# Expert tiles of a fused decoder layer: gate and up product with the weights held and the tokens moving

## The reference

```python
combine = (one_hot(topk_idx, 16) * topk_w[..., None]).sum(1)      # 4 of 16 experts per token
def step(acc, ew):                                                # per expert, I = 176
    w_gu, w_d, cw = ew                                            # (352, 256), (256, 176), weight per token
    gu = x @ w_gu.T
    h = silu(gu[:, :176]) * gu[:, 176:]
    return (acc + h @ w_d.T * cw[:, None], None)
```

## Time and profile before

| | |
|---|---|
| median of 3 runs | 620.12 us |
| profiled execution, its own time | 620.9 us |
| its span, first to last instruction | 619.1 us |
| TensorE matmul busy (PE) | 582.2 us, 94% |
| weight loads (PEld) | 457.3 us, 74% |
| VectorE (DVE) | 492.9 us, 80% |
| ScalarE (ACT) | 415.8 us, 67% |
| POOL | 396.7 us, 64% |
| mean granted TensorE clock | 0.986 of full speed |

### The profile page before, as it was taken

One profiled execution on the slowest core, in us unless ns is written; L12 is line 12 of the kernel. 1 busy time (PEld: TensorE's weight loads), 2 busy tenths in 40 slices (PEclk: granted clock), 3 DMA queues, 4 the chain that ended last, 5 costly groups with the idle time before them and its releaser, 6 DMA issues.

```text
span 619.1 us, 18771 instructions
## 1 busy us (share of the span) xinstructions
PE 582.2 (94%) x5883; PEld 457.3 (74%) x5883; DVE 492.9 (80%) x1516; ACT 415.8 (67%) x1060; POOL 396.7 (64%) x439
## 2 busy tenths in 40 slices
PE   7789899999999999999999999978899999999991
PEld 2558779889888897898888888966467667676760
DVE  4558798989979989899878768577567789989883
ACT  4877977877868768878678586432266666666661
POOL 1147868888888878878788878696100456545553
PEclk9999999999999999999999999899899999999996
DMA  7826324334233233153202111012444677877753
GB/s 228 281 78 179 104 87 137 87 104 155 80 128 106 82 123 115 67 158 113 100 2 96 45 44 53 19 35 87 145 120 137 179 222 217 238 220 226 225 164 115
DMA packets 55682, 78.95 MB, mean 128 GB/s; under 512 B 7330, under 2 KB 46370, under 8 KB 55588
## 3 DMA queue, kind: packets, MB, share of 16 engines
q1 hardware_dynamic: 37300, 48.51, 25.9%
q0 software_dynamic: 6912, 18.88, 10.2%
q10 hardware_dynamic: 11376, 10.36, 4.9%
HBM read 44.43 MB, written 33.29 MB: 126 GB/s over the span
## 4 chain that ended last, share of the span: by engine, by line
PE 81%; POOL 6%; issue 6%; ACT 2%; DVE 2%; DMA 1%; POOLq 0%; DVEq 0%; ACTq 0%
PE ps L776 11%; PE ps L660 9%; PE ps L555 7%; PE ps L588 6%; PE ps L486 5%; PE ps L682 5%; PE ps L788 5%; PE ps L799 4%; PE ps L543 4%; PE ps L608 4%; PE ps L592 3%; PE ps L765 3%; PE ps L526 2%; POOL kv_lo L1491 2%; PE ps L516 2%
## 5 line engine op out<-in xcount | busy, mean ns | idle before, releaser
L1491 POOL TENSOR_TENSOR kv_lo<-kv,kv_hi 128x512 f16<-128x512 f32 x64 | 79.6, 1245 | 30.2 <-ACT kv_hi L914 29.9
L1562 POOL DMA_INDIRECT toeplitz_lo<-y_slots,slots x44 | 43.3, 983 | 81.3 <-DMA y_slots<-kv 57.3
L776 PE MATMUL ps<-w_gate_up_hi,toeplitz_hi 128*128 x316 | 83.6, 313 | 0.4 <-DVE toeplitz_hi L1399 0.4
L1530 POOL DMA_INDIRECT x_slots<-x_norm,slots x64 | 69.2, 1080 | 18.8 <-issue 14.4
L1479 POOL TENSOR_TENSOR kv<-ctx_t_sb,v_t 128x512 f32<-128x512 f32 x64 | 69.2, 1091 | 15.9 <-ACT v_t L903 15.8
L883 ACT ACTIVATE probs<-ps,row_neg_max 128x128 f32<-128x128 f32 x256 | 71.8, 393 | 1.1 <-DVE row_neg_max L1091 0.9
L555 PEld LDWEIGHTS ps<-v_ones,probs_t 128*128 128x128 f32 x512 | 62.2, 192 | 2.2
L555 PE MATMUL ps<-v_ones,probs_t 128*128 128x17 f32 x512 | 60.7, 256 | 0.0
L588 PE MATMUL ps<-kv_hi,toeplitz_hi 128*128 128x128 f16 x256 | 56.5, 221 | 3.2 <-POOL kv_lo L1491 1.7
L1000 ACT ACTIVATE toeplitz_hi<-ps 128x256 f16<-128x256 f32 x79 | 30.3, 384 | 43.4 <-ACT stage L1019 17.9
L588 PE MATMUL ps<-kv_lo,toeplitz_hi 128*128 128x128 f16 x256 | 56.3, 220 | 0.0
(11 more groups left out here) (226 smaller groups left out, 2074.8 us busy)
## 6 DMA issues: line engine op xcount, KB each, us to landing
stage<-in_w_units SPq DMA_DIRECT2D x36, 512.0 KB, 3.8
x_slots<-zeros SPq DMA_DIRECT2D x15, 512.0 KB
toeplitz_hi<-x_slots SPq DMA_DIRECT2D x40, 128.0 KB
y_slots<-stage ACTq DMA_DIRECT2D x40, 128.0 KB
y_slots<-kv ACTq DMA_DIRECT2D x39, 128.0 KB
kv_hi<-x_slots SPq DMA_DIRECT2D x20, 128.0 KB
x_slots<-zeros SPq DMA_DIRECT2D x1, 2432.0 KB
kv_lo<-x_slots SPq DMA_DIRECT2D x19, 128.0 KB
```

The source lines that it names most:

```text
L776: last = nc.tensor.matmul(psum[2 + t % 2][:, 0:2 * INTER], bxT[a][t % 2][:, kc, :], egu[b][:, bass.ds(e, 1), kc, :].rearrange("p a n -> p ...
L1491: nc.gpsimd.tensor_tensor(flat(kvh[1][g % 2]), kv[g % 2][:].rearrange("p h j i -> p (h j i)"), flat(kvh[0][g % 2]), ALU.subtract).then_inc ...
L1530: pool.indirect_dma_start(out=xbuf, out_offset=bass.IndirectOffsetOnAxis(ap=slots[:, row, j:j + 1], axis=0), in_=xn[2][row % 2][:], in_off ...
L1562: pool.indirect_dma_start(out=yg[n][j], out_offset=None, in_=ybuf[0:(last_tile(row, j) + 1) * P], in_offset=bass.IndirectOffsetOnAxis(ap=s ...
```

## The change

Gate and up are made the other way round: the weights are held and the tokens move, so that the inner index lies on the partitions and `turn_inner` goes. The 352 weight columns of an expert are laid out anew on the host as gate 0 to 111, up 0 to 111, up 112 to 175, gate 112 to 175, and are used as three held blocks of 112, 128 and 112 columns, each against 2 chunks and 3 products: 18 matmuls of 128 moving columns. The gate goes through the Silu function on ScalarE in two instructions; VectorE multiplies with up in two instructions and writes to PSUM, from which the split in halves goes on as before. The inner index 112 to 175 stands there twice, on partitions 0 to 63 and 64 to 127, since the down product takes these rows once with the high and once with the low weights. The orders of ScalarE and VectorE are turned: the split of tile s-2 now stands ahead of the gate of tile s-1. A Silu of one column is put ahead of the stage on ScalarE.

```diff
@@ gate_up, turn_inner, down_tile (TensorE)
                 e = experts[t]
-                for kc in range(KC):
-                    for a, b, first, end in products(kc == 0, kc == KC - 1):
-                        last = nc.tensor.matmul(psum[2 + t % 2][:, 0:2 * INTER], bxT[a][t % 2][:, kc, :],
-                                                egu[b][:, bass.ds(e, 1), kc, :].rearrange("p a n -> p (a n)"),
-                                                start=first, stop=end)
+                to = psum[2 + t % 2]
+                for at, n, col in ((0, IN_A, 0), (2 * IN_A, 2 * IN_B, P), (IN_A, IN_A, 2 * P)):
+                    for kc in range(KC):
+                        for a, b, first, end in products(kc == 0, kc == KC - 1):
+                            last = nc.tensor.matmul(to[0:n, col:col + P],
+                                                    egu[b][:, bass.ds(e, 1), kc, at:at + n].rearrange("p a n -> p (a n)"),
+                                                    bxT[a][t % 2][:, kc, :], start=first, stop=end, skip_group_check=True)
                 last.then_inc(t_gu.sem, 1)
-
-            def turn_inner(t):
-                if t < 2:
-                    emptied(4 + t)
-                t_inner.wait(pe, t)
-                t_hlo.wait(pe, t - 2)
-                to, h = psum[4 + t % 2], bhh[t % 2]
-                for c in range(2):
-                    last = nc.tensor.transpose(to[:, c * P:(c + 1) * P], h[:, c * P:(c + 1) * P], id_sb[:])
-                last.then_inc(t_hT.sem, 1)
...
-                for piece, behind in ((turn_x, 0), (gate_up, 1), (turn_inner, 2), (down_tile, 3)):
+                for piece, behind in ((turn_x, 0), (gate_up, 1), (down_tile, 3)):
@@ ScalarE
+            nc.scalar.activation(sink[:], minus_half[:], ACT.Silu)
...
-                t_ga.wait(act, t - 2)
-                nc.scalar.activation(bth[t % 2], psum[2 + t % 2][:, 0:INTER], ACT.Tanh, scale=0.5 / WS)\
-                    .then_inc(t_th.sem, 1)
+                t_inner.wait(act, t - 2)
+                if t == 0:
+                    act.wait_ge(s_set, 14)
+                to, g = bsg[t % 2], psum[2 + t % 2]
+                nc.scalar.activation(to[0:IN_B, 0:P], g[IN_B:P, P:2 * P], ACT.Silu, scale=1.0 / WS)
+                nc.scalar.activation(to[0:IN_A, P:2 * P], g[0:IN_A, 0:P], ACT.Silu, scale=1.0 / WS).then_inc(t_sg.sem, 1)
...
-                for piece, behind in ((x_hi, 0), (gate_th, 1), (inner_hi_tile, 2), (y_out, 3)):
+                for piece, behind in ((x_hi, 0), (inner_hi_tile, 2), (gate_silu, 1), (y_out, 3)):
@@ VectorE (the three instructions of gate_tile go)
+            def inner_tile(t):
...
+                t_sg.wait(dve, t)
+                t_hlo.wait(dve, t - 2)
+                to, g, sg = psum[4 + t % 2], psum[2 + t % 2], bsg[t % 2]
+                nc.vector.scalar_tensor_tensor(out=to[0:IN_A, 0:2 * P], in0=g[0:IN_A, P:3 * P], scalar=1.0 / WS,
+                                               in1=sg[0:IN_A, :], op0=ALU.mult, op1=ALU.mult).then_inc(t_in.sem, 1)
+                t_in.wait(dve, t)
+                nc.vector.scalar_tensor_tensor(out=to[IN_B:P, 0:P], in0=g[0:IN_B, P:2 * P], scalar=1.0 / WS,
+                                               in1=sg[0:IN_B, 0:P], op0=ALU.mult, op1=ALU.mult).then_inc(t_inner.sem, 1)
...
-                for piece, behind in ((x_lo, 0), (gate_tile, 1), (inner_lo_tile, 2)):
+                for piece, behind in ((x_lo, 0), (inner_lo_tile, 2), (inner_tile, 1)):
```

More of the change, by code:

```diff
@@ L21 @@
 EXPERTS, TOP, INTER, SHARED = 16, 4, 176, 704
+IN_A, IN_B = 112, 64
 NB = 16
@@ L251, in build @@
         acc = [st[:, 1024 + n * E:1024 + (n + 1) * E] for n in range(2)] + [z_mem[:, TOP * E:(TOP + 1) * E]]
-        bth = [st[:, 1536 + n * INTER:1536 + (n + 1) * INTER] for n in range(2)]
-        bga = [st[:, 1888 + n * INTER:1888 + (n + 1) * INTER] for n in range(2)]
-        bhh = [st[:, 2240 + n * E:2240 + (n + 1) * E] for n in range(2)]
+        bsg = [st[:, 2240 + n * E:2240 + (n + 1) * E] for n in range(2)]
+        sink = sb("table_sink", [P, 1])
         psum = [stack.enter_context(nc.psum_tensor(f"ps{n}", [P, 512], F32)) for n in range(8)]
@@ L303, in build @@
         down_done, xsh_ready = signal("down_done"), signal("x_shared_ready")
+        s_set = sem("buffers_set")
         s_tab_pe = sem("table_products")
@@ L315, in build @@
         t_xT, t_xhi, t_xlo = signal("tile_x_transposed"), signal("tile_x_hi"), signal("tile_x_lo")
-        t_gu, t_th, t_ga, t_inner = (signal(f"tile_{n}") for n in ("gate_up", "tanh", "gated", "inner"))
-        t_hT, t_hhi, t_hlo = signal("tile_inner_transposed"), signal("tile_inner_hi"), signal("tile_inner_lo")
+        t_gu, t_sg, t_in, t_inner = (signal(f"tile_{n}") for n in ("gate_up", "gate", "inner", "inner_twice"))
+        t_hhi, t_hlo = signal("tile_inner_hi"), signal("tile_inner_lo")
         t_dn, t_y = signal("tile_down"), signal("tile_y")
@@ L798, in down_tile @@
                 for a, b, first, _ in products(True, False):
-                    nc.tensor.matmul(to, bhT[a][t % 2][:, 0, :], eda[b][:, bass.ds(e, 1), :].rearrange("p a n -> p (a n)"),
-                                     start=first, stop=False)
-                nc.tensor.matmul(to, bhT[0][t % 2][:, 1, :], edb[:, bass.ds(e, 1), :].rearrange("p a n -> p (a n)"),
+                    nc.tensor.matmul(to, bhT[a][t % 2][0:IN_A, 1, :],
+                                     eda[b][0:IN_A, bass.ds(e, 1), :].rearrange("p a n -> p (a n)"), start=first, stop=False)
+                nc.tensor.matmul(to, bhT[0][t % 2][:, 0, :], edb[:, bass.ds(e, 1), :].rearrange("p a n -> p (a n)"),
                                  start=False, stop=False)
-                nc.tensor.matmul(to, bhT[1][t % 2][:, 1, :], edb[:, bass.ds(e, 1), :].rearrange("p a n -> p (a n)"),
+                nc.tensor.matmul(to, bhT[1][t % 2][0:IN_B, 0, :],
+                                 edb[0:IN_B, bass.ds(e, 1), :].rearrange("p a n -> p (a n)"),
                                  start=False, stop=True).then_inc(t_dn.sem, 1)
             for s in range(TILES + 3):
-                for piece, behind in ((turn_x, 0), (gate_up, 1), (turn_inner, 2), (down_tile, 3)):
+                for piece, behind in ((turn_x, 0), (gate_up, 1), (down_tile, 3)):
                     if 0 <= s - behind < TILES:
@@ L1001, in x_hi, with gate_silu @@
                     .then_inc(t_xhi.sem, 1)
-            def gate_th(t):
+            def gate_silu(t):
                 t_gu.wait(act, t)
-                t_ga.wait(act, t - 2)
-                nc.scalar.activation(bth[t % 2], psum[2 + t % 2][:, 0:INTER], ACT.Tanh, scale=0.5 / WS)\
-                    .then_inc(t_th.sem, 1)
+                t_inner.wait(act, t - 2)
[4 more added lines that the diff above has]
+                nc.scalar.activation(to[0:IN_A, P:2 * P], g[0:IN_A, 0:P], ACT.Silu, scale=1.0 / WS).then_inc(t_sg.sem, 1)
             def inner_hi_tile(t):
-                t_hT.wait(act, t)
+                t_inner.wait(act, t)
                 t_dn.wait(act, t - 2)
@@ L1333, in _ @@
             table_after = {"ix": round_tiles, "hl1": mark_tiles, "fin": copy_table}
-            s_set = sem("buffers_set")
             for n in range(2):
@@ L1390, in _ @@
             for n in range(2):
-                nc.vector.memset(bhh[n][:, P:], 0.0).then_inc(s_set, 1)
+                nc.vector.memset(bsg[n][:, 0:P], 0.0).then_inc(s_set, 1)
             dve.wait_ge(s_set, 14)
@@ L1400, in x_lo @@
                                         bxT[0][t % 2].rearrange("p c n -> p (c n)"), ALU.subtract).then_inc(t_xlo.sem, 1)
[L1402 to L1413, removed]
+            def inner_tile(t):
+                if t < 2:
+                    for use, _ in BANKS[4 + t]:
+                        READER[use][0].wait(dve, NB - 1, READER[use][1])
+                t_sg.wait(dve, t)
[6 more added lines that the diff above has]
+                                               in1=sg[0:IN_B, 0:P], op0=ALU.mult, op1=ALU.mult).then_inc(t_inner.sem, 1)
             def inner_lo_tile(t):
@@ L1633, in weight_units @@
     units += list(down.reshape(2, 3, P, E).transpose(0, 2, 1, 3))
-    egu = a["L0_ffn_expert_gate_up"].reshape(EXPERTS, 2 * INTER, KC, P).transpose(0, 3, 2, 1)
+    gate, up = np.split(a["L0_ffn_expert_gate_up"], 2, axis=1)
+    egu = np.concatenate([gate[:, :IN_A], up[:, :IN_A], up[:, IN_A:], gate[:, IN_A:]], axis=1)
+    egu = egu.reshape(EXPERTS, 2 * INTER, KC, P).transpose(0, 3, 2, 1)
     units += list(egu)
     ed = a["L0_ffn_expert_down"].transpose(2, 0, 1)
[L1637 to L1640, removed]
+    first = np.zeros((P, EXPERTS, E), np.float32)
+    first[0:IN_A] = ed[0:IN_A]
+    units += [first[:, q:q + QUADS] for q in range(0, EXPERTS, QUADS)]
+    rest = np.concatenate([ed[IN_A:], ed[IN_A:]], axis=0)
     units += [rest[:, q:q + QUADS] for q in range(0, EXPERTS, QUADS)]
```

## The result

The changed kernel takes 713.24 us (median of 6 runs, 712.73 to 718.36), the kernel before 618.64 us (median of 6). The ratio is 1.154, with a 95% interval of 1.149 to 1.159: slower by 15%. The prediction said slower, 679 us, with a range of 641 to 706. The direction and the bound were right, the size was not: 34 us lie above the forecast and 7 above the range.

What follows compares the result with a forecast made beforehand. The prediction took TensorE's sequencer as the bound; +1.0 - 0.2 - 0.04 = +0.76 us per step made 2.80 us, times 78 +59 us, so 679 us, with a range of 641 to 706.

Steps and rivals of the forecast that it cites:

- The bound: Tile stage before the change: TensorE's sequencer, feeding instructions to the array, sets the 2.04 us step; the array is slightly shorter.
- Address groups, +1.0 per step: Gate products on TensorE's sequencer: six groups of address arithmetic instead of two, 0.25 us each, +1.0 us per step (+0.8 to +1.2).
- turn_inner gone, -0.2: TensorE's sequencer between load check and down arithmetic: one wait and two transposes go, -0.2 us per step (0 to -0.4).
- The table load: Expert number's load on TensorE's sequencer, started at 473.6 with its check ending after 474.1: 0.5 us of the step, kept unchanged.
- Array, 1.80: TensorE's array after the change: 1.03 us for 18 matmuls, transposes less 0.22, sum 1.80 us per step, hidden behind the sequencer.
- Turned orders, no bound: ScalarE's and VectorE's new order in the stage: 4.4 us for two steps, 2.2 each, so it does not limit the step.
- Rival A: Gate products' weight loads of 112 columns set the array's pace: step 2.31 us, 641 us; chance 0.06.
- B: Sequencer's address work hides behind the busy array, so array and VectorE decide: step about 1.91 us, 611 us; chance 0.09.
- C: TensorE's clock falls to half and stays because the array idles a third of the time: 743 us; chance 0.04.
- D: ScalarE swaps its function table in every tile, two loads of 1.28 us: 4.2 us per step, 790 us; chance 0.03.

## Why the prediction was wrong, point by point

- **The bound: right.** That TensorE's sequencer paces the kernel before was read from the pause ahead of L788 and from its absence in the last step. Both halves were shown: taken out of the kernel before, the sequencer's work gave back 12 us; put in by the cut into three blocks, it cost 97.
- **Address groups, +1.0 per step: right.** Six groups, 1.5 us for the block.
- **turn_inner gone, -0.2: inside its bounds, 0.07 too much.** From the end of the table load to the down product's arithmetic the median tile took 0.58 us before and takes 0.45 now: -0.13.
- **The table load: the step that failed.** The prediction listed it in the 0.5 us between 473.6 and 474.1, and carried it unchanged into the new step. In the mean of all tiles it went from 0.324 to 0.677 us: +0.35 of the 0.44 us by which the step exceeded 2.80. Times 78 this is 28 of the 34 us missed, and moving the load or the store brought 26 back. (The medians, 0.30 and 0.72, would give 32; they overstate it, since some loads were long before and some are short after.) The prediction gives no reason for holding it still: the edit does not touch the load, but it moves it. What it should have asked: the load's place relative to ScalarE's store moves when the block ahead of it grows by 1 us; what will it then collide with? The trace of before had nine loads over 0.4 us, up to 0.600, which one step does not show. They would have told that the load's time is not fixed, but not what lengthens it: none of them stood within 1.4 us behind a store's issue.
- **With the load free of the store** the forecast's step of 2.80 stands against 2.88 and 2.87, and its 679 us against 687 in both runs. The rest, 0.07 per step, is as much as `turn_inner` fell short of its -0.2; the gate block is 1.0 us longer, as forecast.
- **Array, 1.80: wrong by 0.2, hidden.** Measured 2.02 with a free sequencer. The gate products were right, 1.00; the 64-row product (0.20 before it, 0.21 behind) was taken at 0.11, as all of the earlier trace rows. It cost nothing here, but it means that without any sequencer cost the change brings nothing: 621 us against 618 for the kernel before as it is, and against 607 for the kernel before with its sequencer freed in the same way.
- **Turned orders, no bound: right here, for the reason given.** Freed of the sequencer and of the 64-row product, their loop sets a step of 1.98 us, less than the 2.2 estimated, but more than the array.
- **Rival A, slow loads of 112 columns: refuted.** Their weight load has a median of 0.129 us against 0.098 for 128 columns, yet with the array full products start 0.056 apart. The Trainium skill, "TensorE: Matmul & The Clock Gate", section on weight-path perf modes, has fast weight load on only when the number of weights is 128, and the longer record agrees with that. The 93 ns that the prediction estimated from its LDWEIGHTS section does not show as the pace of the products.
- **Rivals B, C, D: refuted.** B: the six groups hold the sequencer for 1.5 us and the array waits, and even without the sequencer's cost the change only ties; the clock stayed at 1.00 in both stretches, with PE busy 13.8 of 20 us; the trace of after has one further function table load, ahead of the stage.

## What to carry to other kernels

Where operands are addressed through a register, count the distinct addresses per step and price each as sequencer time, about 0.25 us here for one pair and its three products, before counting matmul columns: a product cut in three costs the array some 0.1 us per step (18 products 1.00 us, six 0.90) and cost the kernel 97 us in all. Read the sequencer's rows as a bound of their own when an engine waits for nothing. And when an edit shifts a step by a microsecond, look at what short, untouched operations will land beside; read their spread over the whole run, not one instance, and multiply by their mean, not by their median.

## What the runs showed of the hardware that was not expected

- A sequencer's load of one number from SBUF takes 0.30 us, but 0.72 (median, up to 0.81) when it starts about 0.4 us after the issue of a 128 KB store from SBUF has ended while tiles are also loaded, and 0.55 when none is. Beyond 0.6 us after the store's issue most loads are back at 0.30. Moving load or store returned it to 0.30. By which path the two meet is open; a run with a narrower store was not made.
- A load of four numbers takes 0.336 us, hardly more than one of one, and 0.742 beside the store.
- A held operand of 64 rows between operands of 128 puts 0.20 us ahead of and 0.21 behind its product of 256 columns, where full rows have 0.11; one of 112 rows does not.
- The best version found is the kernel before with four numbers per load and no check of bounds: 608.2 us, 1.6% below the kernel before.
